# An output projection rewritten as Strassen block products, eight cores

## The reference

```python
x = layernorm(x + ssm(x, Wi, Wo, A_log, Wb, Wc, Wdt, b_dt, Wg))     # state-space layer
h = x * rsqrt(mean(x * x) + EPS) * w_norm
gv = act_quant(h) @ weight_quant(w_gv).T       # 2048 -> 2 * 8192
value, gate = split(gv, 2)
u = value * silu(gate)
out = act_quant(u) @ weight_quant(w_out).T     # 8192 -> 2048
x = layernorm(x + (x + out))
```

## Time and profile before

| | us |
|---|---|
| times of three runs | 3056.54, 3203.9 (median), 3415.42 |
| profiled execution, its time | 3054.91 |
| its span on the slowest core | 3053.3 |
| spans of the eight cores | 3034.4 to 3053.3 |
| TensorE busy, share of the span | 88% |
| VectorE, ScalarE, GpSimd busy | 63%, 54%, 16% |

### The profile page before, as it was taken

One profiled execution on the slowest core, in us unless ns is written; L12 is line 12 of the kernel. 1 busy time (PEld: TensorE's weight loads), 2 busy tenths in 40 slices (PEclk: granted clock), 3 DMA queues, 4 the chain that ended last, 5 costly groups with the idle time before them and its releaser, 6 DMA issues.

```text
span 3053.3 us, 36798 instructions; the slowest of 8 cores (3034.4 to 3053.3 us)
## 1 busy us (share of the span) xinstructions
PE 2698.2 (88%) x12080; PEld 1199.2 (39%) x12080; DVE 1910.0 (63%) x2015; ACT 1642.3 (54%) x1964; POOL 500.8 (16%) x364
## 2 busy tenths in 40 slices
PE   3555621899999999999999999999899999999998
PEld 1112210344444444444444444444344444444444
DVE  3688985777777787768677777777452332432421
ACT  2677874667777767778888888886010100100000
POOL 1222100322222222313232222220000000000000
PEclk9778755899999999999999999999999999999999
DMA  9999999799999999889989898997862342332420
GB/s 310 330 326 323 322 327 341 202 213 219 222 216 226 214 211 221 217 192 242 234 237 234 228 248 231 235 229 222 269 208 86 107 141 83 119 130 83 134 94 28
DMA packets 264957, 645.29 MB, mean 211 GB/s; under 512 B 17920, under 2 KB 165424, under 8 KB 239680
## 3 DMA queue, kind: packets, MB, share of 16 engines
q1 hardware_dynamic: 173232, 523.29, 61.1%
q10 hardware_dynamic: 88608, 101.21, 12.9%
...
...
## 4 chain that ended last, share of the span: by engine, by line
PE 65%; DMA 13%; DVE 9%; issue 6%; ACT 5%; SPq 1%; POOL 1%; ACTq 1%; DVEq 0%; POOLq 0%
PE pvg L867 36%; PE pvg L1090 25%; DMA ring<-wgvt 8%; DVE wop L772 2%; PE pvg L1111 2%; DMA ringb<-wgvt 2%; ACT ring L801 2%; DMA ring<-u_sp 1%; DMA ringb<-xq 1%; DVE ub L907 1%; DVE sg L902 1%; ACT sn L882 1%; DVE sg L915 1%; SPq L1052 1%; ACT ring L255 1%
## 5 line engine op out<-in xcount | busy, mean ns | idle before, releaser
L867 PE MATMUL pvg<-q,wop 128*128 128x512 f16 x4096 | 951.0, 380 | 6.7 <-ACT wop L762 3.5
L758 POOL TENSOR_SCALAR ring<-ring,wsc 128x1024 f32<-128x1024 f32 x254 | 408.0, 1609 | 1269.4 <-DMA ring<-wgvt 1120.3
L867 PEld LDWEIGHTS pvg<-q,wop 128*128 128x128 fp8e4 x4096 | 401.5, 98 | 494.2 <-issue 15.5
L882 ACT COPY sn<-pvg 128x512 f32<-128x512 f32 x512 | 293.9, 581 | 256.8 <-PE pvg L867 215.4
L1090 PE MATMUL pvg<-qob,Tb 128*128 128x512 fp8e4 x1920 | 418.9, 380 | 5.0 <-DMA qob<-qo_sp 5.0
L1175 ACT ACTIVATE pvg<-Ta 128x2048 f32<-128x2048 f32 x15 | 28.2, 1882 | 700.8 <-DVE Ta L1171 649.1
L867 PE MATMUL pvg<-Ta,wop 128*128 128x512 f16 x1536 | 362.8, 379 | 12.5 <-ACT sn L882 8.8
L867 PE MATMUL pvg<-Tb,wop 128*128 128x512 f16 x1536 | 364.5, 380 | 1.2 <-ACT sn L882 1.2
L1090 PEld LDWEIGHTS pvg<-qob,Tb 128*128 128x128 bf16 x1920 | 187.7, 98 | 234.3 <-issue 9.4
L1171 DVE SCALAR_TENSOR_TENSOR Ta<-pvg,c2c,Ta 128x2048 f32<-128x2048 f32 x15 | 35.3, 2351 | 386.1 <-PE pvg L1090 386.1
L902 DVE TENSOR_TENSOR sg<-pvg,sn 128x1024 f32<-128x1024 f32 x128 | 156.8, 1225 | 169.7 <-PE pvg L867 113.3
...
## 6 DMA issues: line engine op xcount, KB each, us to landing
ring<-woutT SPq DMA_DIRECT2D x256, 512.0 KB, 6.3
ring<-wgvt SPq DMA_DIRECT2D x252, 512.0 KB, 8.8
...
u_sp<-ub ACTq DMA_DIRECT2D x128, 512.0 KB, 8.7
ring<-u_sp SPq DMA_DIRECT2D x128, 512.0 KB, 6.0
...
qo_sp<-qo_t ACTq DMA_DIRECT2D x128, 128.0 KB, 8.0
```

The costliest lines, as they stand in the source:

```text
L758: t = eng.do(lambda e: e.tensor_scalar(out=ap, in0=ap, scalar1=wsc[:, 1:2], scalar2=MAGIC, op0=ALU.mult, op1=ALU.add))
L867: t_pr[(n, name)] = pe.do(lambda e, k=k, w=w, m=m, o=o, first=first: e.matmul(o, w[:, k * 128:(k + 1) * 128], m[:, k * TS:(k + 1) * TS], s ...
L882: t_sn[(n, name)] = ac.do(lambda e: e.copy(out=sn[:, i * TS:(i + 1) * TS], in_=bank(h, b)))
```

## The change

The output projection becomes 64 groups. A group G is one pass over half of the output columns (`dp`), one pair of token tiles (`v`) and a quarter of the hidden rows (`g`). Its operands are four 128x1024 blocks of u. `load_u` fetches them from `u_sp` into four single buffers, a block as soon as the buffer's last rounding is done. `mult` scales them on VectorE, `rounds` rounds them on ScalarE (four additions of the constant, then four subtractions to fp16), `asums` forms S1 to S4 on VectorE. `group` does seven products of eight matmuls, each on a bank of its own, accumulated over the four g of a tile pair; `wo_y` adds the state-space output by four matmuls a pair. After g = 3, `combos` puts the banks together on the residual: ScalarE copies P1's bank, VectorE has nine additions onto the residual and three between banks, all 512 columns wide; `squares` follows on ScalarE. As each tile pair is seen in two passes, u is read twice, the first pass's half of the residual goes to HBM (`r_sp`) and comes back, and `normal` runs in the second pass only: some ten small instructions, and the scaling of four 128x1024 blocks, two on VectorE and two on ScalarE.

In value and gate, `tern_o` makes two blocks into a tile with the seven operands of w_out: GpSimd does four 128x512 fp8 subtractions and issues one store of 448 KB, where ScalarE issued one of 128 KB per block. The ring of half buffers has four instead of five.

```diff
-    NHALF = 5
+    NHALF = 4
...
-    def tern_o(i):
-        s, ap, tok = half_load(osrc(i))
+    def tern_o(k):
+        p, r = divmod(k, 2)
+        dp, j = divmod(p, HC // 2)
+        s, ap, tok = half_load(osrc(2 * (j + r * HC // 2) + dp))
         ac.wait(tok, t_so[0], t_magp)
         t = ac.do(lambda e: e.activation(out=ap, in_=ap, func=AF.Identity, scale=wsc[:, 4:5],
                                          bias=magp[:]))
-        if i >= 1:
-            store_o(i - 1)
-        ac.wait(t, t_os.get(i - NO))
-        t_qo[i] = ac.do(lambda e: e.activation(out=qo_t[:, (i % NO) * 1024:(i % NO + 1) * 1024],
-                                               in_=ap, func=AF.Sign, bias=magn[:],
-                                               saturate=False))
-        hfree[s].append(t_qo[i])
-
-    def store_o(i):
-        ac.wait(t_qo[i])
-        t_os[i] = ac.dma(oslot[i % NO], lambda e: e.dma_start(
-            out=qo_sp[i // 2][:, (i % 2) * 512:(i % 2 + 1) * 512],
-            in_=qo_t[:, (i % NO) * 1024:(i % NO + 1) * 1024].bitcast(BF16)))
+        ac.wait(t, t_os.get(p - NO))
+        tile = qo_t[:, (p % NO) * 7 * TS:(p % NO + 1) * 7 * TS]
+        t_qo[k] = ac.do(lambda e: e.activation(out=tile[:, r * 1024:(r + 1) * 1024], in_=ap,
+                                               func=AF.Sign, bias=magn[:], saturate=False))
+        hfree[s].append(t_qo[k])
+        if r == 1:
+            b = lambda i: tile[:, i * TS:(i + 1) * TS]
+            tt = lambda o, u, v: po.do(lambda e: e.tensor_tensor(
+                out=b(o), in0=b(u), in1=b(v), op=ALU.subtract, saturate=False))
+            po.wait(t_qo[k - 1], t_qo[k])
+            t1 = tt(4, 1, 0)
+            t3 = tt(6, 3, 1)
+            po.wait(t1)
+            t2 = tt(5, 3, 4)
+            po.wait(t2, t3)
+            po.wait(tt(1, 2, 5))
+            t_os[p] = po.dma(oslot[p % NO], lambda e: e.dma_start(
+                out=wq_sp[dp, j // 8][:, (j % 8) * 1792:(j % 8 + 1) * 1792],
+                in_=tile.bitcast(BF16)))
...
+    def load_u(G):
...
+        for k, (a, b) in enumerate(PARTS):
+            sp.wait(t_A2.get((G - 1, k)))
+            t_ust[(G, k)] = sp.dma(stslot[k], lambda e, k=k, a=a, b=b: e.dma_start(
...
+    def mult(G):
...
+            dv.wait(t_ust[(G, k)], t_s2b[0 if i < 8 else 2 + (i - 8) // 4])
+            t_mul[(G, k)] = dv.do(lambda e, u3=u3, sc=sc: e.tensor_tensor(
+                out=u3, in0=u3, in1=sc, op=ALU.mult))
...
+    def rounds(G):
...
+        for k in range(4):
+            uc = ring[:, k * 1024:(k + 1) * 1024]
+            ac.wait(t_mul[(G, k)], t_magp)
+            t_add[(G, k)] = ac.do(lambda e, uc=uc: e.activation(
+                out=uc, in_=uc, func=AF.Identity, bias=magp[:]))
+        for k, (a, b) in enumerate(PARTS):
+            name = f"A{a + 1}{b + 1}"
+            uc = ring[:, k * 1024:(k + 1) * 1024]
+            ac.wait(t_add[(G, k)], t_pd.get((G - 2, USER[name])), t_A2.get((G - 2, "S4")),
+                    t_rows[0] if G == 0 else t_pr[(NSET - 1, "P5")] if G == 1 else None)
+            t_A2[(G, k)] = t_A2[(G, name)] = ac.do(lambda e, uc=uc, name=name: e.activation(
+                out=a2(G, name), in_=uc, func=AF.Identity, bias=magn[:]))
+    def asums(G):
...
+        def tt(o, x, y, op):
+            dv.wait(t_pd.get((G - 2, USER.get(o, "P5"))))
+            t_A2[(G, o)] = dv.do(lambda e: e.tensor_tensor(out=a2(G, o), in0=a2(G, x),
+                                                           in1=a2(G, y), op=op))
+            return t_A2[(G, o)]
+        dv.wait(*(t_A2[(G, k)] for k in range(4)))
+        t = tt("S3", "A11", "A21", ALU.subtract)
+        dv.wait(t)
+        t = tt("S1", "A21", "A22", ALU.add)
+        dv.wait(t)
+        t = tt("S2", "S1", "A11", ALU.subtract)
+        dv.wait(t)
+        tt("S4", "A12", "S2", ALU.subtract)
...
+    SEQ = (("P1", "A11", 0), ("P2", "A12", 2), ("P6", "S2", 5), ("P7", "S3", 6), ("P5", "S1", 4),
+           ("P4", "A22", 1), ("P3", "S4", 3))
...
+    def group(G):
...
+        for n, (name, an, w) in enumerate(SEQ):
+            pe.wait(t_A2[(G, an)])
+            if g == 0:
+                pe.wait(t_fr.get((G // 4 - 1, name)))
+                if G == 0 and n == 4:
+                    pe.wait(t_x[NSET - 1], t_y[NSET - 1])
+                if name in YB:
+                    wo_y(G, name, False)
+            for j in range(8):
+                if v == 0 and j % 4 == 0:
+                    pe.wait(t_w[(dp, g, j // 4)])
+                o = (j * 7 + w) * TS
+                t_pd[(G, name)] = pe.do(lambda e, j=j, o=o, an=an, name=name: e.matmul(
+                    bk2(name), a2(G, an)[:, j * 128:(j + 1) * 128], wgr[g][:, o:o + TS],
+                    start=(g == 0 and j == 0 and name not in YB), stop=(g == 3 and j == 7)),
+                    count=(j == 7))
+        if g == 3:
+            wo_y(G, "Y", True)
...
+    def combos(V):
...
+        def add(a, b, src, tok, last=False):
...
+            t_r[(V, a, b)] = dv.do(lambda e: e.scalar_tensor_tensor(
+                out=ltap(V, a, b), in0=src, scalar=c2c[:, i:i + 1], in1=ltap(V, a, b),
+                op0=ALU.mult, op1=ALU.add, **kw))
+            return t_r[(V, a, b)]
+        def tt(o, x, y, *toks):
+            dv.wait(*toks)
+            t = dv.do(lambda e: e.tensor_add(out=o, in0=x, in1=y))
             dv.wait(t)
...
+            return t
+        pd = lambda name: t_pd[(G, name)]
+        fr = lambda name, t: t_fr.__setitem__((V, name), t)
+        t_c = ac_copy(V, u3)
+        fr("P1", t_c)
+        add(0, 0, u3, t_c)
+        fr("P2", add(0, 0, bk2("P2"), pd("P2"), True))
+        fr("P6", tt(u2, bk2("P6"), u3, pd("P6")))
+        fr("P7", tt(u3, bk2("P7"), u2, pd("P7")))
+        tt(u2, bk2("P5"), u2, pd("P5"))
+        add(1, 1, u3, None)
+        fr("P5", add(1, 1, bk2("P5"), pd("P5")))
+        fr("P4", add(1, 0, bk2("P4"), pd("P4")))
+        add(1, 0, u3, None, True)
+        fr("P3", add(0, 1, bk2("P3"), pd("P3")))
+        add(0, 1, u2, None, True)
+        fr("Y", add(1, 1, bk2("Y"), t_Y[(G, "Y")], True))
+    def ac_copy(V, o):
+        ac.wait(t_pd[(4 * V + 3, "P1")], t_r.get((V - 1, 1, 0)))
+        t = t_fr[(V, "P1c")] = ac.do(lambda e: e.copy(out=o, in_=bk2("P1")))
+        return t
...
+    def squares(V):
...
+            t_sq2[(V, a)] = ac.do(lambda e, a=a, i=i: e.activation(
+                out=sqd, in_=ltap(V, a), func=AF.Square,
+                accum_out=acco[:, 16 * dp + i:16 * dp + i + 1]))
...
+    for G in range(3, NG):
+        dp, v, g = split(G)
+        V = G // 4
+        load_u(G + 1)
+        if g == 1 and V > 1:
+            load_lt(V)
+        if g == 1 and dp == 1:
+            load_rh(V)
+        group(G)
+        if v == 7 and dp == 0:
+            sp.wait(t_pd[(G, "P3")])
+            load_w(1, g)
+            if g == 3:
+                sp.wait(t_Y[(G, "Y")])
+                load_wo2(1)
+        mult(G + 1)
+        rounds(G + 1)
+        if g == 3:
+            combos(V)
+        asums(G + 1)
+        if g == 3:
+            squares(V)
+            if dp == 1:
+                normal(V)
+        if g == 2 and V > 1:
+            scale_lt(V)
```

More of the change, by code:

```diff
@@ L1325, in build_program @@
-    last_tile()
-    sp.wait(t_out[NT - 2], t_out[NT - 3])
+    load_w(0, 3)
+    load_u(3)
+    sp.wait(t_red[1])
+    load_lt(0)
+    scale_lt(0)
+    mult(3)
+    rounds(3)
+    group(2)
+    asums(3)
+    t_row[0] = late_row(0, 0, None)
+    for G in range(3, NG):
+        dp, v, g = split(G)
+        V = G // 4
[22 more added lines that the diff above has]
+            scale_lt(V)
+        if 4 <= G < 7:
+            t_row[0] = late_row((G - 3) // 2, (G - 3) % 2, t_row[0])
+        if G == 6:
+            sp.wait(t_row[0])
+            load_lt(1)
+            scale_lt(1)
```

403 lines of the change are left out of this document (208 added, 195 removed).

## The result

The changed kernel takes 3532.2 us in its profiled execution, against 3056.5 before. The ratio is 1.155, 95% interval 1.150 to 1.160 (executions in which the cores of a die ran at a lower clock are left out, which leaves one of the changed kernel and two of the kernel before). The forecast was 3240, its range 3140 to 3345. The verdict "slower" was right; between the two profiled executions the loss is 477 us instead of 185.

The account below looks back on a forecast made before the run. Before, TensorE bounds the kernel; after, VectorE and ScalarE take over in the output projection, undoing TensorE's gain of 110 us. 3054.9 + 148 (output projection) + 37 (value and gate) = 3240 us, range 3140 to 3345, held at about 0.8.

Parts of the forecast that it names:

- +37 us: Value and gate, last units: GpSimd's subtractions and store delay its scaling, so TensorE waits 1.2 us at 31 places.
- its bound of +102: Value and gate: the loss in us if a GpSimd subtraction takes 1.63 us, making the wait 3.3 us.
- plain cycle: Output projection: preparing a group without a pair's end takes 13.16 us, 13.5 with late loads, against TensorE's 12.07.
- pair's end: Output projection, 15 tile pairs: copy and `combos` overlap no matmuls of their pair, adding 10.0 us to 13.16.
- the start, group 0 to 4: Output projection: 68 us instead of 53 for four cycles, with the last unit's VectorE work between.
- the end: Output projection, from the last group's first addition: rounding, matmuls, last additions, squares, statistics, scaling and store, 33 us.
- the forecast's last case: Whole kernel: the clock or a stall of another kind, above 3350 us, chance 0.03.
- the signs that the prediction named for its mechanism: After 2200 us: VectorE and ScalarE at 6 tenths or more, 13 to 14 us cycles, TensorE waiting for sums.
- its signs of being wrong: Output projection: TensorE waits for nothing, or its waits are for loads, or a plain cycle is below 12.5 us.
- `combos` hides after all: Rival, output projection: the 10 us at each of 15 pairs don't appear; 3090 us, chance 0.08.
- The loads set the pace: Rival, output projection: loads of u land after 8.8 us instead of 6.8; 3328 us, chance 0.12.
- TensorE's clock falls: Rival, output projection: granted clock 0.50, 3700 us if it stayed; chance 0.03 shared with other stalls.

Follow-up runs that it names:

- e3_copy_first: Changed kernel with ScalarE's copy of P1's bank moved ahead of the next group's roundings in the output projection; 3446.3 us, ratio 1.130.

## Why the prediction was wrong

**The step that failed** is value and gate: "TensorE waits 1.2 us. There are 31 such places: +37 us", outside even its bound of +102. In a place of the milder kind TensorE waited 5.4 us, in one of the other kind 8.15, and there are 30 places, since the last four units all make w_out ternary. Four things were wrong in the sum.
- It let GpSimd start on the second tile when the last sign ended, and so counted four subtractions. A `tern_o` unit makes two tiles, and GpSimd was 2.6 us behind with the first. From the end of the last sign to ScalarE's next one it took 9.9 us (1812.25 to 1822.16), not 6.8 (1520.4 to 1527.2).
- It took the last sign 1.4 us earlier, because ScalarE no longer issues four stores. That gain did not come. The rows of before (below) show the issue beside a running activation, and the signs come 2.43 us apart (1518.26, and 1520.69 in the earlier trace rows); in the changed kernel they come 2.37 apart (the last at 1811.10). Measured against the time when P5 is wanted, the last sign is only about 0.1 us earlier than in the earlier trace rows.
- The price of a subtraction was about right for one by itself (least 1.086 us, taken 1.1). Here they took 1.52 in the mean, since VectorE's reads hold them up; in every second place that adds 2.8 us. The page cited ahead (the Trainium skill, "GPSIMD Engine Reference", section 3.1) gives 1.11 us; the least duration agrees, the mean does not.
- The clock was priced at nothing. That was said of the output projection, but each of the 30 long stalls in value and gate is followed by matmuls at the 1.2 GHz level: the next eight start over 3.0 to 3.4 us instead of 1.7. In the window from 1340 us to value and gate's end, TensorE was busy for 837.6 us; in the kernel before, 774.6 for as many matmuls: 63 us.

The rows of the second point, before and after:

```profile
1516.89 1.22 ACT L801 ACTIVATE ring<-ring,magp,wsc 128x1024 f32<-128x1024 f32 x1
1517.06 0.36 ACTq L813 DMA_DIRECT2D qo_sp<-qo_t  x1
1518.26 1.15 ACT L806 ACTIVATE qo_t<-ring,magn 128x1024 fp8e4<-128x1024 f32 x1
```

```profile
1808.73 1.15 ACT L810 ACTIVATE qo_t<-ring,magn 128x1024 fp8e4<-128x1024 f32 x1
```

With the forecast's own 37 us the first three come to about 37 + 30 x 2.6 + 30 x 1.3 + 15 x 2.8 = 196 (an estimate from these rows). In that window TensorE idled 210.9 us, 15.4 before: 195.5 more, and with the 63 that is the 258. The runs divide the same loss another way: of 260 us by the medians, spreading the tiles takes 108 off, the buffers 21, the subtractions' reading 55; 64 stay for GpSimd's occupied time and what isn't told apart from it, and 11 for the rest of the change.

The trace of before already spoke of the stretched instructions, in rows that I did not weigh. Groups by form, 1340 to 2130 us:

```profile
L758 POOL TENSOR_SCALAR ring<-ring,wsc 128x1024 f32<-128x1024 f32 x120 | 194.6, 1624 | 556.6 <-DMA ring<-wgvt 556.4
L772 DVE TENSOR_TENSOR wop<-wop 128x1024 fp8e4<-128x1024 fp8e4 x62 | 105.1, 1696 | 6.8 <-DVE wop L772 0.5
...
L772 DVE TENSOR_TENSOR wop<-wop,wa 128x1024 fp8e4<-128x1024 fp8e4 x30 | 36.5, 1218 | 0.0
```

The same sum takes 1.22 us in one place and 1.70 in another, and the scaling of 1.12 us 1.62 in the mean. The Trainium skill ("SBUF — State Buffer", section "Who interferes with whom") says that a VectorE instruction with two SBUF inputs contends with a GpSimd instruction that reads SBUF, not with one that only writes it, and that the order of issue decides which of the two blocks. By that rule L927 can stretch and L914, with a bank as one input, must not, and fills must not stretch anything: all three agree (up to 4.67 us; 1.22 to 1.23; 0.69 and 1.28 beside fills).

**The output projection** was right in its mechanism, and most of its terms in size: plain cycle 13.16 forecast, 13.32 measured; pair's end 23.16 and 22.88 (that most of what it has over a plain cycle, 6.1 of 9.6 us, comes from the copy's place is shown by e3_copy_first); with `normal` 27.16 and 27.3. Of the 71 us missing in 1070:
- the start, group 0 to 4, took 82.5 us instead of 68 (L1212 waited 13.87 us for its load, ahead of a rounding in ScalarE's queue);
- one more such wait (11.0 us) made the step into group 8 22.6 us instead of 13.5;
- the change of pass took 28 us more over groups 30 to 33: eight loads of 1.8 MB stand in SyncE's queue beside those of u, and VectorE waited up to 16.0 us;
- the end took 40 us instead of 33, and the other 40 plain cycles 13.74 instead of 13.5, 10 us.

**The rivals.** The measured time lies in the forecast's last case, a stall of another kind, above 3350, which got 0.03. In the output projection the signs that the prediction named for its mechanism were seen (but for VectorE and ScalarE, which are at 5 tenths as often as at 6), and none of its signs of being wrong. "`combos` hides after all" got 0.08 and was false: it starts only after the copy. "The loads set the pace" got 0.12 and was true only in part: in places in the changed kernel, and in the second pass once the ring is opened. "TensorE's clock falls" got 0.03 and was true in half of its text: the granted clock was 0.90 in both stages, not 0.50. That in the output projection most of this lies beside VectorE's work is argued and not tested; in value and gate it doesn't. That the change wins (0.05) was far off.
